# Reordering the event list of a pipelined local transformer

## The reference, cut to what matters

```python
def attn_layer(x, Wqkv, qs, ksc, Wo):          # 16 heads of 64
    q, k, v = split(x @ Wqkv)                  # (b, heads, 256, 64)
    q = l2norm(q) * qs
    k = l2norm(k) * ksc
    q = q * cos * scale + rotate_half(q) * sin * scale
    k = k * cos / scale + rotate_half(k) * sin / scale
    out = local_attention(q, k, v)             # each window sees itself and the one before
    return out @ Wo
def ffn_layer(x, g, bln, W1, b1, W2, b2):
    xn = layernorm(x) * g + bln
    a, gate = split(xn @ W1 + b1)
    return a * gelu(gate) @ W2 + b2
for i in range(6):
    x = attn_layer(shift_tokens(x), ...) + x
    x = ffn_layer(shift_tokens(x), ...) + x
```

## Time and profile before

| what | value |
|---|---|
| median of three runs | 4301.71 us (4296.09 to 4313.28) |
| profiled execution: own time / span | 4313.28 us / 4311.5 us |
| PE busy in the span | 3548.9 us (82%) |
| DVE, ACT, POOL busy | 2647.6, 1984.4, 1213.6 us |
| the sublayer that changes, from 2519 to 3553 us | 1034 us |
| in it: PE, DVE, ACT, POOL busy | 926.6, 740.3, 574.9, 514.2 us |
| mean granted PE clock, whole span / this stage | 0.891 / 0.97 |

### The profile page before, as it was taken

The page is one execution under the profiler, slowest core; times in us unless marked ns, Lnnn a source line. Parts: engine busy times, 40 slices in busy tenths (PEclk is TensorE's granted clock), DMA queues, the critical chain, the costliest instruction groups (busy, mean ns, idle before and its releaser), DMA issues. The chain is left out here.

```text
span 4311.5 us, 96137 instructions
## 1 busy us (share of the span) xinstructions
PE 3548.9 (82%) x40572; PEld 2381.5 (55%) x40572; DVE 2647.6 (61%) x4567; ACT 1984.4 (46%) x3507; POOL 1213.6 (28%) x813
## 2 busy tenths in 40 slices
PE   7565788999999977799377669989999976699996
PEld 4445555777777757223122345656666654466773
DVE  4134484666666662788755857777777755565663
ACT  1131344555555544588501235555555552245552
POOL 1102104555555534000000445555545530200000
PEclk9576788999999988899798879999999997789997
DMA  1023200000000008000001010000000000100000
GB/s 37 5 65 92 99 1 36 9 1 9 1 1 1 1 8 269 18 1 1 1 5 42 23 57 18 13 23 24 13 18 12 2 2 17 31 18 18 10 2 10
DMA packets 73830, 109.24 MB, mean 25 GB/s; under 512 B 14434, under 2 KB 56090, under 8 KB 72636
## 3 DMA queue, kind: packets, MB, share of 16 engines
q1 hardware_dynamic: 70396, 96.86, 7.5%
q0 software_dynamic: 3008, 6.23, 0.4%
HBM read 86.37 MB, written 10.94 MB: 23 GB/s over the span
## 5 line engine op out<-in xcount | busy, mean ns | idle before, releaser
L1990 PE MATMUL narrow_ps_t<-narrow_Q,narrow_KQ 32*128 32x256 f32 (+2 forms) x2176 | 397.0, 410 | 6.2 <-ACT narrow_probsT L2076 3.0
L2076 ACT ACTIVATE narrow_probsT<-narrow_ps_t 128x512 f32<-128x512 f32 (+1 forms) x448 | 232.9, 566 | 225.8 <-PE narrow_ps_t L1990 223.5
L2549 POOL TENSOR_TENSOR wide_probs<-wide_probs,wide_factor 128x1024 f32<-128x1024 f32 x128 | 239.6, 1893 | 311.4 <-ACT wide_factor L2510 311.4
L2506 ACT ACTIVATE wide_probs<-wide_ps_s,wide_nm 128x1024 f32<-128x1024 f32 (+1 forms) x256 | 237.2, 927 | 173.2 <-DVE wide_nm L2591 153.1
L1990 PEld LDWEIGHTS narrow_ps_t<-narrow_Q,narrow_KQ 32*128 32x128 f32 (+1 forms) x2176 | 281.1, 191 | 46.7 <-ACT narrow_probsT L2076 21.6
L2953 PE MATMUL bonds_ps<-bonds_act_of,bonds_out 128*32 128x448 f32 (+3 forms) x1024 | 281.6, 567 | 24.8 <-ACT bonds_rows L2936 18.5
L2126 DVE TENSOR_REDUCE narrow_part<-narrow_ps_s 128x1 f32<-128x512 f32 x384 | 236.0, 682 | 106.3 <-PE narrow_ps_s L1973 106.3
L3525 POOL TENSOR_TENSOR local_turn<-local_turn 128x1024 f32<-128x1024 f32 x96 | 226.9, 2364 | 248.7 <-DVE local_turn L3583 248.7
L1973 PE MATMUL narrow_ps_s<-narrow_KQ 32*128 32x512 f32 x768 | 256.2, 678 | 35.7 <-DMA narrow_KQ<-narrow_close 18.8
L2586 DVE TENSOR_REDUCE wide_nm<-wide_ps_s 128x1 f32<-128x1024 f32 x128 | 155.9, 1219 | 193.6 <-PE wide_ps_s L2392 193.6
L2902 DVE TENSOR_TENSOR bonds_strain<-peri_in_moved 128x1664 f32<-128x1664 f32 (+3 forms) x128 | 257.3, 2085 | 5.8 <-ACT bonds_act_of L2925 5.1
(11 more groups left out here) (597 smaller groups left out, 8103.9 us busy)
## 6 DMA issues: line engine op xcount, KB each, us to landing
moe_w<-in_L_ffn_w SPq DMA_DIRECT2D x62, 512.0 KB, 4.8
local_wqkv<-in_L_ffn_qkv SPq DMA_DIRECT2D x6, 1536.0 KB, 6.7
context_rows<-in_ctx SPq DMA_DIRECT2D x8, 768.0 KB
context_keys<-in_ctx_T SPq DMA_DIRECT2D x6, 800.5 KB, 4.3
narrow_KQ<-narrow_close SPq DMA_DIRECT2D x64, 58.0 KB
wide_source<-in_ctx_T SPq DMA_DIRECT2D x4, 800.5 KB, 4.2
narrow_source<-in_ctx_T SPq DMA_DIRECT2D x4, 800.5 KB, 4.4
local_wo<-in_L_ffn_out SPq DMA_DIRECT2D x6, 512.0 KB, 4.2
```

The lines of the kernel that those rows point to most:

```text
L1990: mm = pe.matmul(bank[0:hi - lo, at:at + q1 - q0], KQ_of(s)[part_of(h), lo:hi], Q2[part_of(h), s % RING, q0:q1], start=True, stop=True, sk ...
L2076: act.activation(probsT[0:high, c % PROBS, h, 0:wide], bank[0:high, 0:wide], ACT.Exp).then_inc(t_taken_act.sem, 1)
L2506: act.activation(probs[:, n % 2, h, lo:hi], ps_s[h][:, 0:hi - lo], ACT.Exp, bias=nm[:, n % 2, h, 2 * half:2 * half + 1], scale=1.0, accum_ ...
L2549: pool.tensor_tensor(v, v, factor[:, n // 4 % 2, j:j + 1].broadcast_to([P, CUT]), ALU.mult).then_inc(lowered[i].sem, 1)
```

## The change

The list is put in another order, which is the order of every engine's queue. Within a round va now stands ahead of exp and k; k stands behind pt and ga; vb stands behind s; gv moves up to k; gx, ga and gb stay in their rounds. gd moves from the odd round behind that of ga and gb into the same even round, behind vb. xs stands at the start of the odd round. The list gets one round shorter. The event sum is gone: DVE adds the squares right behind its rotary products of k. The preload of the Ln and Exp table moves from root to directly behind the Gelu of gb, in every round that has one.

```diff
-        for r in range(ROUNDS + 7):
-            yield from [("q", r), ("kt", r - 1), ("exp", r - 2), ("k", r), ("va", r)]
-            if r % 2:
-                shift, last = (r - 5) // 2, (r - 7) // 2
-                yield from [("gm", shift), ("pt", r - 2), ("gd", last), ("qt", r - 1), ("sum", r), ("ot", r - 3), ("xs", last),
-                            ("root", r), ("vb", r), ("gv", shift), ("s", r - 1), ("rest", r), ("wo", r - 3), ("o", r - 2), ("gx", shift)]
-            else:
-                g = (r - 6) // 2
-                yield from [("pt", r - 2), ("ga", g), ("gb", g), ("qt", r - 1), ("sum", r), ("ot", r - 3), ("root", r), ("vb", r),
-                            ("s", r - 1), ("rest", r), ("wo", r - 3), ("o", r - 2), ("sh", (r - 4) // 2)]
+        for r in range(ROUNDS + 6):
+            yield from [("q", r), ("xs", (r - 7) // 2 if r % 2 else -1), ("kt", r - 1), ("va", r), ("gm", (r - 5) // 2 if r % 2 else -1),
+                        ("exp", r - 2), ("pt", r - 2), ("ga", (r - 6) // 2 if r % 2 == 0 else -1), ("k", r),
+                        ("gb", (r - 6) // 2 if r % 2 == 0 else -1), ("gv", (r - 5) // 2 if r % 2 else -1), ("qt", r - 1), ("ot", r - 3),
+                        ("root", r), ("s", r - 1), ("gx", (r - 5) // 2 if r % 2 else -1), ("rest", r), ("vb", r),
+                        ("gd", (r - 6) // 2 if r % 2 == 0 else -1), ("wo", r - 3), ("o", r - 2), ("sh", (r - 4) // 2 if r % 2 == 0 else -1)]
...
-                    if ("ga", (n - 6) // 2) in rank and n % 2 == 0:
-                        act.preload_act_table_set("natural_log_exp_and_others")
...
                     a.then_inc(gelu_ready.sem, 1)
+                    if kind == "gb":
+                        act.preload_act_table_set("natural_log_exp_and_others")
...
                     dve.tensor_tensor(turn2[:, j, :, 32:], v[:, :, 0:32], factor(1, 32, 64), ALU.mult).then_inc(taken_dve.sem, 1)
-                elif kind == "sum":
-                    for side in range(2):
-                        dve.tensor_reduce(ss[:, n % 2, side, :], sq[:, side, :, :], AX.X, ALU.add)
-                    dve.drain()
-                    dve.tensor_scalar(ss[:, n % 2, :, :], ss[:, n % 2, :, :], 1e-24, None, ALU.max).then_inc(ss_ready.sem, 1)
+                    if j:
+                        for side in range(2):
+                            dve.tensor_reduce(ss[:, n % 2, side, :], sq[:, side, :, :], AX.X, ALU.add)
+                        dve.drain()
+                        dve.tensor_scalar(ss[:, n % 2, :, :], ss[:, n % 2, :, :], 1e-24, None, ALU.max).then_inc(ss_ready.sem, 1)
```

## The result

| | before | after |
|---|---|---|
| median | 4304.87 us (4 runs) | 4419.64 us (4 runs, 4402.02 to 4431.37) |
| ratio | 1 | 1.0283, 95% interval 1.0256 to 1.0308 |
| profiled execution, own time / span | 4313.28 / 4311.5 us | 4408.29 / 4406.5 us |
| stage, from the first q on PE to the transposes behind the last layer | 1025.3 us | 1138.8 us |
| PE busy / idle in the stage | 925.5 / 99.8 us | 930.4 / 208.4 us |

The kernel is 115 us slower by the medians, against a forecast of 98. The stage took 113.5 us longer, 104.1 of it in the 42 rounds that the forecast counted. The two profiled executions differ by less, since the parts that did not change ran 18 us shorter in the second. Executions of the changed kernel that were made later, beside the experiments, took 4414 to 4440 us.

A forecast was written before the change was run, and what follows sets the result against it. PE was taken to bound the stage. New idleness of 133 us less the old 54 gave +79, and the clock 19 more: +98 us, 4400 against the median (4411 against the profiled execution). Range 4325 to 4460.

The forecast's parts named there:

- The bound: PE bounds the changed stage, 41.6 us a pair of rounds; an order can change only its idle time, 72.8 us.
- The old waits: PE's waits ahead of gd (37.3 us) and gb (16.6 us) for DVE's products of k: all 53.9 us would go.
- The exp behind va: In ACT's queue exp follows V's copy, so pt on PE waits 2.1 us in even rounds, 1.45 in odd.
- The second gap: Even round: s on PE waits 1.15 us for ACT's copy of qt, which stands behind the second table load.
- the lower end: Second gap with the table load free: s would still wait 0.75 us for k's slot.
- The third gap: Even round: vb on PE waits 1.15 us for gb's slot, since DVE's part of gb follows the sums.
- The square between two Gelus: ACT's square of k was taken to need no table load; with two loads more a pair, 21 us in all.
- The odd round, s: Odd round: s on PE waits 0.5 us for ACT's copy of qt, which ends at 7.85.
- The clock: PE's clock falls after waits, 0.24 us lost per us of idleness: 19 us more; lower end nothing, upper end 52.
- The move of xs: xs at the start of the odd round comes earlier than its reader, the next even q, needs it: no cost.
- the first and last rounds: Exp gap in the first rounds, at most 8 us; table loads saved in the last, at most 4: together zero.
- the first rival: Clock falls to 0.92: 4433 us; if gx on DVE also sits out two POOL instructions, 4452. Chance 0.12.

The follow-up runs named there:

- c2: The changed kernel with the table preload back at root: 4449.6 us, ratio 1.0319 to the kernel before.
- a1: The changed kernel with exp ahead of va again: 4397.16 us, ratio 1.022 to the kernel before.
- a5: The changed kernel with exp ahead of va and xs back behind ot: 4375.08 us, ratio 1.014 to the kernel before.
- a3: The kernel before with exp moved behind va, directly ahead of pt: 4330.53 us, ratio 1.0062.
- g1: The kernel before with exp directly ahead of pt, and k behind pt in odd rounds, behind pt and ga in even ones: 4399.12 us, ratio 1.0185.
- a4: The changed kernel with exp ahead of va, sums behind gb, preload at root and xs behind ot: 4353.53 us, ratio 1.0116 to the kernel before.
- l1: The changed kernel with vb ahead of s again: 4455.93 us, ratio 1.0336 to the kernel before.
- b1_v_early: The kernel before with vb directly behind va, ga ahead of pt in even rounds, gd ahead of gm in odd ones: 4277.02 us, ratio 0.9934.

## Why the prediction was right, and where not

- **The bound.** PE set the stage, and the time followed its idle time: +108.6 of +113.5 us.
- **The old waits** went, all of the 53.9 us. Right.
- **The exp behind va.** Right to 0.03 us: 2.07 and 1.44 measured for 2.1 and 1.45, 73.7 us in the 21 pairs for 75, and 83.4 in the whole stage for 83.
- **The second gap, s behind the table load:** 1.20 for 1.15, 27.3 us for 24. c2 showed that the load is not what one would gain by undoing: k's slot comes free almost as late, after 1.12 us where the lower end had 0.75. The square between two Gelus took no load. The table load held ACT for 1.28 us, and the next instruction started 0.02 behind its end, as in the earlier trace rows. The Trainium skill ("ScalarE: Activation LUTs", What ACT_TABLE_LOAD costs) gives 2.66 us for a switch, and my estimate by that figure had the even round 1.2 us longer; the traces do not agree with it.
- **The third gap, vb behind the sums:** right in kind, 17.4 us for 24. It appears in 14 of 21 rounds. In the timeline above the pause within s covers it: DVE's part of gb ended during that pause.
- **The odd round, s.** This step failed. It said "copies qt until 7.85: s waits 0.5", and the wait is 1.50, for k's slot. I had worked out the reader of k's slot for the even round and left it out for the odd one, where it is s as well. By the prediction's own durations k is squared until 5.95 and its products end 2.4 later, at 8.4, 1.05 behind ot; the trace has 1.5 because ot follows sooner than I counted and PE starts 0.15 behind the release. The term was 10.5 us and measured 31.6. That is the larger part of what the forecast lacks.
- **The clock.** 19 us forecast, 1.9 us more busy time measured in the same 42 rounds, 4.9 in the stage (925.5 to 930.4). The ratio of 0.24 us lost per us of idleness did not hold here: the mean granted clock of the stretch fell from 0.98 to 0.97, but that mean takes in the idle time too, and the busy time hardly followed. In the runs the busy time of the same 16273 matmuls of the stage lies between 902 and 949 us; it is lowest in the four fastest kernels, but does not follow the idle time closely (946 in a1 with 161 us idle, 930 in the changed kernel with 208).
- **The move of xs** was put at nothing, and in the changed kernel it cost PE nothing that shows. But its copy took 2.49 us in all 20 cases, against 0.29 before, and a1 and a5 show that this cost was only hidden behind the wait for exp.
- **The pauses.** I had no term for them. They rose from 16.2 to 24.9 us in the stretch. The traces show what they are. The profile's list of DMA queues has a queue of the kind "instruction", with 325 packets of 16 KB in either kernel:

```profile
q8 instruction: 325, 5.32, 0.5%
```

If one counts the instructions of PE with its weight loads and its sequencer's, all 379 pauses over 0.15 us in the stages of the 14 traces fall on one grid of 256 instructions, to within two, while the waits for other engines do not (15 of 1209 do). Each pause ends 1.2 to 1.6 us after such a packet has landed, and at the grid points without a pause the packet had landed 1.2 us ahead or more. In the timeline above the packet took from 3336.31 to 3337.42, and PE went on at 3338.93. So in a pause PE waits for its next block of instructions. The 128 matmuls of s, with 128 weight loads, use up 256 instructions in 1.5 us.

- **The sum.** In the 42 rounds waits grew by 94 us and pauses by 9, against 79 and none: too low by 24. The clock was 17 too high. These two nearly cancel, so that the forecast of 98 lies close to the 104.1 measured there by luck in part. The other 9.4 us of the stage came in the first and last rounds, which I had put at zero, between 4 us less and 8 more.
- **What the parts cost.** The prediction lists the waits rightly but for k's slot in the odd round; yet a list of waits is not a list of what undoing each part would bring. The exp wait was its largest term (75 of 133 us), and undoing it in the changed kernel brought 0.6%, since gv took over; with xs back behind ot as well it brought 1.4%. Added alone to the kernel before it cost 0.6% too, since the same event took DVE's row sums out of k's way. The larger step is k behind pt and ga: from a3 to g1 the ratio goes from 1.006 to 1.019, and with the exp in its old place (a4) the new order of PE costs 1.2%. The rest up to 1.028 is not pinned to one part: undoing the sums brought 0.1%, which is within the noise, and undoing the preload or vb's place brought nothing. The places of gd and gv were not tried alone.

**Open.** The pauses sum to between 19 and 53 us a stage. A new order of the list puts other work at the grid of 256 instructions, but when the chip starts to fetch a block, and so which order makes it late, no run here shows. The busy time, too, varies without an account. In the profiled executions c2 has 14 us more of pauses and 18 more of busy time than the changed kernel, which makes most of the 34 us by which its stage is longer; l1 has 17 more of pauses, of 18 in all. In l1 the unchanged parts were also at their longest, 3310 us, and no run shows why.

## What to carry to other kernels

Where one list orders the queues of all engines, moving an event moves its work on each of them, also on the engine where that hurts or helps unseen: follow every engine's part before pricing a move. With buffers dealt out in turn, find the reader of each buffer after every reordering, in every kind of round, and count the work between the last use and that reader. And when a wait names a late engine, look first at what stands ahead of the late instruction in its queue and is not needed yet: moving 1.7 us of row sums on DVE brought 1.3%, against 0.7% for the new order of PE that was tried for the same waits (b1_v_early).

## What was unexpected of the hardware

A copy of 64x255 elements on DVE (L3641) took 2.49 us when POOL's addition of 128x1024 started with it, and 0.29 us when POOL was idle. The changed order moved such collisions about rather than removing them: the copy of xs (L3645 before) went from 0.29 to 2.49 each time, the copy of sh (L3618 before, 0.29 to 1.82 us) now takes 0.29 in the median, the scaling in gx (L3627 before) 0.48 instead of 2.04, while the addition behind it (L3625 after) takes 1.83 instead of 0.35. The Trainium skill ("SBUF — State Buffer", Who interferes with whom) says that a VectorE copy in one of its two-port modes and a GpSimd instruction cannot run together, and that the one that issues first keeps the shared ports for its whole instruction. The times in a1 agree with it: POOL's addition started 0.01 us ahead of the copy, and the copy ended 0.14 us after it. Which mode the copy ran in no run shows. The case of the first rival, that gx sits out two instructions of POOL, did not come: its scaling and addition together took 2.3 us, and one instruction of POOL there took 1.9 to 2.1.

The other is the pauses of PE, told above: a stretch of small matmuls can use up its instructions faster than new ones land. The longest pause in the changed kernel is 4.3 us.
